# Flamingo block on Trainium2: the last key rows of a head group packed two heads to a score bank, the one left-over key apart, and x loaded turned

## The reference

```python
# x (8, 512, 256), ctx (8, 1601, 256), 16 heads of 16 channels
q, k, v = heads(layernorm(x) @ Wq.T), heads(ctx @ Wk.T), heads(ctx @ Wv.T)
attn = einsum('bhnc,bhlc->bhnl', q / 16, k)        # 512 queries x 1601 keys
attn = softmax(attn, axis=2)                       # over the QUERIES n, not the keys
attn = attn / attn.sum(axis=-1, keepdims=True)     # then over the keys
x = x + tanh(g_xattn) * (einsum('bhnl,bhlc->bhnc', attn, v) @ Wo.T)
# feed-forward: 8 experts, the best two of each token, hidden 1024, exact gelu
x = x + tanh(g_ffn) * moe(layernorm(x), router_w, w1, w2)
```

## Time and profile before

| | before |
|---|---|
| median of 3 runs | 1796.7 us (1795.38 to 1799.1) |
| the profiled execution, its own time | 1794.36 us |
| its span in the trace | 1792.6 us |
| busy PE, DVE, ACT, POOL over the span | 95%, 79%, 72%, 30% |
| attention, first exp to last exp | about 31 to 1230 us |
| one batch (2nd to 7th) | 151.3 us |
| granted TensorE clock | 0.996 |

### The profile page before, as it was taken

How to read it: one execution, slowest core, us unless ns; L and a number is a source line. 1 busy time by engine, 2 the same in 40 slices (tenths; PEclk the granted TensorE clock), 3 DMA queues, 4 the chain that set the end, 5 groups by cost and what they waited for, 6 DMA issues and landing times.

```text
span 1792.6 us, 31795 instructions
## 1 busy us (share of the span) xinstructions
PE 1703.8 (95%) x10074; PEld 918.3 (51%) x10074; DVE 1417.2 (79%) x2293; ACT 1283.0 (72%) x3653; POOL 538.2 (30%) x821
## 2 busy tenths in 40 slices
PE   8999999999999999999999999889999999999997
PEld 5233334333333433333333342225899999999997
DVE  7998999999999999999999999997344444444442
ACT  5999999999999999999999999996111111111111
POOL 3331252352343225235223422213122222222222
PEclk9999999999999999999999999999999999999999
DMA  8546226414712721551371163419222222222221
GB/s 231 139 121 183 66 70 158 129 40 123 187 47 62 198 72 52 158 154 40 102 187 51 51 172 75 154 52 326 67 37 35 36 37 35 38 35 35 36 37 27
DMA packets 128247, 172.90 MB, mean 96 GB/s; under 512 B 14496, under 2 KB 105760, under 8 KB 128128
## 3 DMA queue, kind: packets, MB, share of 16 engines
q1 hardware_dynamic: 113152, 150.51, 30.8%
q0 software_dynamic: 14144, 20.44, 6.6%
q10 hardware_dynamic: 832, 0.53, 0.1%
HBM read 117.96 MB, written 53.47 MB: 96 GB/s over the span
## 4 chain that ended last, share of the span: by engine, by line
ACT 40%; PE 30%; DVE 20%; issue 7%; DMA 2%; POOL 1%; SPq 0%; POOLq 0%; DVEq 0%; ACTq 0%
ACT w_all L934 37%; DVE negmax L1114 14%; PE scores L1507 14%; PE scores L1520 13%; ACT w_all L879 1%; ACT parts L870 1%; DVE resid L1009 1%; DMA out<-row_t,gate_token 1%; PE spare L1497 1%; DVE rz L1100 1%; PE scores L732 1%; PE spare L593 1%; DVE x L1025 1%; DVE stats L1133 1%; DVE stats L1143 0%
## 5 line engine op out<-in xcount | busy, mean ns | idle before, releaser
L934 ACT ACTIVATE w_all<-scores,negmax 128x512 f32<-128x512 f32 (+1 forms) x1664 | 1128.9, 778 | 19.9 <-DVE negmax L1114 15.4
L1114 DVE TENSOR_REDUCE negmax<-scores 128x2 f32<-128x1024 f32 (+1 forms) x832 | 1001.9, 1215 | 53.8 <-PE scores L732 47.4
L732 PE MATMUL scores<-q_stack,w_all 128*128 128x512 bf16 (+1 forms) x1664 | 532.9, 385 | 42.1 <-ACT w_all L934 34.3
L934 ACT ACTIVATION_READ_ACCUMULATOR w_all<-scores,negmax 128x1 f32 (+1 forms) x1664 | 495.2, 298 | 0.0
L745 PE MATMUL acc<-w_all,vz 128*32 128x512 f32 (+1 forms) x3328 | 443.7, 605 | 0.0
L732 PEld LDWEIGHTS scores<-q_stack,w_all 128*128 128x128 bf16 (+1 forms) x1664 | 136.8, 99 | 575.2 <-ACT w_all L934 514.6
L1553 ACT ACTIVATE projections<-scores 128x512 f32<-128x512 f32 x142 | 84.8, 597 | 445.8 <-PE scores L1507 440.2
L1337 POOL TENSOR_TENSOR vz<-w_all,rz 128x68 f32<-128x68 f32 (+1 forms) x416 | 124.5, 299 | 776.3 <-DVE rz L1100 751.0
L1507 PEld LDWEIGHTS scores<-row_t,q_stack 128*128 128x128 f32 x2272 | 264.4, 192 | 7.0 <-issue 2.0
L1507 PE MATMUL scores<-row_t,q_stack 128*128 128x128 f32 x2272 | 265.6, 275 | 1.9 <-DVE row_t L1580 1.9
L1520 PE MATMUL scores<-room,projections 128*128 128x256 f32 x1136 | 256.8, 379 | 0.0
(11 more groups left out here) (215 smaller groups left out, 1048.9 us busy)
## 6 DMA issues: line engine op xcount, KB each, us to landing
w_all<-k_parts SPq DMA_DIRECT2D x248, 200.1 KB, 3.5
w_all<-in_w SPq DMA_DIRECT2D x16, 1024.0 KB, 10.0
q_stack<-q_parts SPq DMA_DIRECT2D x248, 64.0 KB, 3.3
k_parts<-parts SPq DMA_DIRECT2D x42, 300.0 KB, 2.9
w_all<-in_ctx_t SPq DMA_DIRECT2D x7, 1601.0 KB, 7.1
parts<-routed SPq DMA_DIRECT2D x71, 129.0 KB
q_parts<-parts SPq DMA_DIRECT2D x14, 384.0 KB, 3.9
routed<-pad_row SPq DMA_DIRECT2D x8, 645.0 KB
```

The source lines that it names most:

```text
L732: mm = pe.matmul(scores[0:r, 2 * (u % SLOTS) + j % 2, :], k_stacks[g][:, j, lt * P:lt * P + r], q_stack[:, g, j, :], start=True, stop=True)
L934: act.activation(probs[0:r, s % RING, j, :], scores[0:r, 2 * (u % SLOTS) + j % 2, :], ACT.Exp, bias=negmax[0:r, u % 4, j % 2:j % 2 + 1], a ...
L1114: dve.tensor_reduce(negmax[0:r, u % 4, :], scores[0:r, 2 * (u % SLOTS):2 * (u % SLOTS) + 2, :], AX.X, ALU.max, negate=True).then_inc(negma ...
```

## The change

It does four things.

1. **Packing.** The last tile now holds 64 rows. A group's 13th step is one unit: the four heads' scores are made by four matmuls with 64 columns, heads 0 and 1 (2 and 3) one above the other in one bank. Key 1600, left over, is put apart for all 16 heads at once: one more unit of one bank (the *lone* unit), in which row 32j + g is head j of group g, made by 16 matmuls with 32 columns. Batch 0 makes it in two parts, at steps 12 and 38, the others in one, at step 12. `weigh` of each 13th step has four more matmuls for it. The numbering of slots runs on over the batches.
2. **Values.** The last v piece (tiles 12 and 13) is made with the new shapes, and DVE takes it with a multiplication by a 0/1 mask (`own_rows`), where ACT copied it. It is now at step 24.
3. **x.** x is given turned as well and loaded so (`x_t`). SP writes means and deviations to DRAM, loads them back on all partitions, and POOL centres and scales `x_t` at steps 24 to 27. The two x_turn pieces are gone.
4. **The table.** Steps 12, 25, 38 and 51 carry no side work. v 0 to 5 stand at 36, 41, 43, 45, 47 and 49. `load_ctx` waits for v 5 (step 49) and no longer for v 6 (step 47).

```diff
-LT = (L + P - 1) // P
+LT = L // P
+LAST_TILE = LT * P
+REST = L - 1 - LAST_TILE
+TAIL_ROWS = 32
+LONE = LAST_TILE + REST
+LONE_AT = LONE + H // 4 - 1
+LK = LONE_AT + TAIL_ROWS
+VT = LT + 2
+GROUP_STEPS = LT + 1
...
 FILL_AT = {
     1: ("next", "k", 0), 3: ("next", "k", 1), 4: ("tail", "o_turn", 3), 5: ("tail", "attn_turn", 1),
...
+    7: ("tail", "out_proj", 0), 9: ("tail", "out_proj", 1), 11: ("next", "k", 2),
+    14: ("next", "k", 3), 16: ("next", "k", 4), 17: ("cur", "o_turn", 0), 18: ("tail", "row_turn", 0),
+    19: ("tail", "row_turn", 1), 21: ("tail", "logits", 0), 23: ("next", "k", 5), 24: ("next", "v", 6),
+    27: ("next", "k", 6), 29: ("next", "k", 7), 30: ("cur", "o_turn", 1), 32: ("next", "q", 0), 34: ("next", "q", 1),
+    36: ("next", "v", 0), 37: ("cur", "attn_turn", 0),
+    39: ("tail", "prefix", 0), 41: ("next", "v", 1), 43: ("next", "v", 2), 45: ("next", "v", 3), 47: ("next", "v", 4),
+    49: ("next", "v", 5), 50: ("cur", "o_turn", 2),
 }
...
+def lone_groups(b, g):
+    if b == 0:
+        return range(g, g + 2) if g % 2 == 0 else range(0)
+    return range(G) if g == 0 else range(0)
+
+def units_of(b, s):
+    g, lt = s // GROUP_STEPS, s % GROUP_STEPS
+    return 2 if lt < LT or len(lone_groups(b, g)) else 1
...
+        def spread_x_stats(it):
+            b = it.b
+            sp.wait_ge(rstd_step, 2 * (b + 2))
+            for s, stat in ((0, mv1[:, :, 0]), (1, rstd1[:, 1, :])):
+                sp.dma_start(x_stats_dram[s].rearrange("(t p) -> p t", p=P), stat, allow_slow_non_contiguous=True).then_inc(x_stats_stored, 16)
+
+        def gather_x_stats(it):
+            b = it.b
+            wait_apart(sp, x_stats_stored, 32 * (b + 1), passed_sp)
+            sp.dma_start(x_stats[:, :, :], x_stats_dram.partition_broadcast(P)).then_inc(x_stats_in, 16)
...
         def load_ctx(it):
 
-            sp.wait_ge(fill_taken, it.made("v", VF - 1))
+            sp.wait_ge(fill_taken, it.made("v", VF - 2))
             sp.dma_start(ctx_sb[:, :, :], ctx_rows[it.b + 2]).then_inc(ctx_loaded, 16)
...
+            elif p == 0:
+                for j in range(GH):
+
+                    wait(pe, exp_done, 2 * (u - SLOTS) + j // 2 + 1)
+                    mm = pe.matmul(scores[REST * (j % 2):REST * (j % 2 + 1), bank + j // 2, :],
+                                   k_stacks[g][:, j, LAST_TILE:LAST_TILE + REST], q_stack[:, g, j, :], start=True, stop=True)
+            else:
+                groups = lone_groups(b, g)
+
+                wait(pe, exp_done, 2 * (u - SLOTS) + 1)
+                for of in groups:
+                    for j in range(GH):
+                        mm = pe.matmul(scores[32 * j:32 * j + TAIL_ROWS, bank, :],
+                                       k_stacks[of][:, j, LONE_AT - of:LONE_AT - of + TAIL_ROWS], q_stack[:, of, j, :],
+                                       start=(of == groups[0]), stop=(of == groups[-1]))
...
+            if lt == LT:
+                pe.wait_ge(lone_vz_ready, lone_units(b, g))
+                for j in range(GH):
+                    mm = pe.matmul(acc[32 * j:32 * j + DH + 1, :], lone_vz[:, g * GH + j, :], lone_probs[:, :],
+                                   start=False, stop=True)
...
+            elif name in ("v", "own_v"):
+                dve.tensor_tensor(v_ones[(b + 1 if name == "v" else b) % 2][:, LT:VT, :, 0:DH],
+                                  spare[:, :].rearrange("p (t h c) -> p t h c", t=2, h=H),
+                                  own_rows[:, :, :].unsqueeze(3).to_broadcast([P, 2, H, DH]), ALU.mult).then_inc(fill_taken, 1)
...
+                if it.next and s in (SHIFT_X, SHIFT_X + 1):
+                    k = s - SHIFT_X
+                    if k == 0:
+                        wait_apart(pool, x_t_loaded, (b + 1) * 16, passed_pool)
+                        pool.wait_ge(x_stats_in, (b + 1) * 16)
+                    pool.tensor_tensor(x_t[:, k, :], x_t[:, k, :], x_stats[:, 0, :], ALU.subtract).then_inc(centred1, 1)
```

More of the change, by code:

```diff
@@ L54 @@
 KCHUNK = 4
-KCOLS = [(L * i) // KCHUNK for i in range(KCHUNK + 1)]
+KCOLS = [(LK * i) // KCHUNK for i in range(KCHUNK + 1)]
 KCMAX = max(KCOLS[i + 1] - KCOLS[i] for i in range(KCHUNK))
 CHUNKS = KC + KC * KCHUNK
-VF = (LT + 1) // 2
+VF = VT // 2
 TOKENS = B * N
@@ L111 @@
 CENTRE_X = 17
+SHIFT_X = 24
 class Iteration:
@@ L649, in fill @@
                 wait(pe, fill_taken, it.made(name, i) - 1)
-            if name == "x_turn":
-                pe.wait_ge(xn_ready, 2 * (b + 2))
-                mm = turn_x(spare, i)
-            elif name == "q":
+            if name == "q":
+                if i == 0 and 0 in halves:
+                    pe.wait_ge(xn_ready, 2 * (b + 2))
                 mm = project_q(spare, i, halves)
@@ L952, in _ @@
         dve.wait_ge(dve_setup, DVE_SETUP)
+        own = Chain(dve, own_rows_step, 0)
+        own(dve.memset(own_rows[:, :, :], 0.0))
+        own.settle()
+        own(dve.memset(own_rows[0:REST, 0, 0::2], 1.0))
+        own(dve.memset(own_rows[REST:P, 0, 1::2], 1.0))
+        for g in reversed(range(G)):
+            for j in range(GH):
+                own(dve.memset(own_rows[32 * j:32 * j + g + 1, 1, g * GH + j:g * GH + j + 1], 1.0))
+            own.settle()
+            if g:
+                for j in range(GH):
+                    own(dve.memset(own_rows[32 * j:32 * j + g, 1, g * GH + j:g * GH + j + 1], 0.0))
+        own.settle()
+        for tiles in v_ones:
+            own(dve.tensor_copy(tiles[:, LT:VT, :, DH], own_rows[:, :, :]))
+        own.settle()
         def bc(ap):
@@ L1125, in run @@
                     f = it.fill(s)
-                    if f and f[0] not in ("v", "own_v", "x_turn") and p == (f[0] in ("q", "k")):
+                    if f and (f[0] not in ("v", "own_v") or f in LAST_V) and p == (f[0] in ("q", "k")):
                         take(it, *f)
```

248 lines of the change are left out of this document (143 added, 105 removed).

## The result

The changed kernel takes 1834.1 us (median of four executions, 1831.8 to 1838.3) where the kernel before took 1796.1 in the same job: a ratio of 1.0208, with a 95% interval of 1.0195 to 1.022. It is 38 us slower. 1783.7 was forecast, with a range of 1766 to 1803, so both the sign and the range were missed. The profiled execution took 1838.29 by its own time, 4.2 above the median, for a span of 1836.6. Against the 1794.4 of before it is 43.9 us longer, and that is the sum to be explained here.

What follows compares the result with a forecast made beforehand. ACT was taken as the bound, with little room behind it. Middle batches -8, first -1.9, last -4.4 and ends +1.2 made -13: 1794.4 to 1781.4, plus 2.3 for the median, 1783.7 us; range 1766 to 1803.

Steps and rivals of the forecast that it cites:

- So 2.0 us of waiting, in each change of batch: Change of batch: context lands at 7.8 us, PE stands from 4.4, ACT waits 2.0 us, at six changes.
- 5 if in 10: Upper end of ACT's wait per change of batch: 5 us if the context load takes 10 us to land.
- the same sign comes if the context takes 10 us to land: Rival at the change of batch: a context landing in 10 us also makes the kernel slower; within slower's 0.19.
- slower: Case that the changed kernel takes longer than before: chance 0.19, of which the lone matmuls 0.10.
- I cost it nothing: Turned x: statistics stored and reloaded through DRAM, bounded by 14 us where POOL has 18, priced at no time.
- 0.35 (0 to 1.1 ...): Step 24: DVE's masked copy of v 6 waits for PE and precedes its second reduce, 0.35 us per batch.
- DVE's sum (0.7): Steps 25 to 30: DVE has some 16.3 us against ACT's 15.3; 0.7 us per batch, between 0 and 1.3.
- the lone key at 28 (0.6): Step 28: the longer `weigh` delays the second unit's scores by a little more than 0.5 us.
- the price of the lone key in `weigh`: Four more matmuls at steps 15, 28, 41 and 2: 1.7 us per middle batch, 0.4 to 4.
- the rival that had them in turn: Step 12: the 16 lone matmuls run one after another, 3.5 us on PE, total 1803; chance 0.10.
- The running slots: Change of batch: slots that run on remove a 0.7 us wait, seven restarts, 4.9 us in all.
- The rival that all waits stay covered (-50): Whole kernel: ACT's saved work and the slot restarts count in full, -50, 1747 us; waits covered had chance 0.21.

Runs made afterwards that it cites:

- a2: Changed kernel with the context loaded in two halves, the first after v 3 and the rest after v 5: 1806.32 us, ratio 1.0051 to the kernel before.
- b1: Kernel before with the turned x alone, without packing or running slots: 1798.99 us against 1795.68, ratio 1.0017.
- b4: Kernel before with v 6 moved from step 47 to 49, so that its context load is issued two steps later: 1805.89 us, ratio 1.0059.
- c1: b2 with the first half of the context issued ahead of the last stack loads in the first batch: 1785.53 us against 1794.62, ratio 0.9952.
- a1: Changed kernel with the fourth group's stack loads waiting until the context has landed: 1826.47 us, ratio 1.0169 to the kernel before.
- a3: Changed kernel with POOL's four operations on the turned x cut from 512 to 8 columns, all waits kept: 1826.42 us, ratio 1.0167 to the kernel before.
- b2: a2 with x by rows and turned by PE as before, and v 6 at step 38 behind its second unit: 1795.49 us, ratio 1.0.
- b3: a2 without the four matmuls that add the lone key in each 13th step's `weigh`: 1793.23 us, ratio 0.9989 to the kernel before.
- c3: Kernel before with only the slots' numbering running on over the batches: 1784.45 us, ratio 0.9946.

## Why the prediction failed

In the profiled execution the sum is off by 57 us (-13 forecast, +43.9 measured). By terms:

| term | forecast | measured | off by |
|---|---|---|---|
| step 0 of the six changes of batch | +12 | +33.7 | 21.7 |
| steps behind them (1 to 3) and single late steps | 0 | +5 | 5 |
| the six batches without both, against 151.3 each | -20 (148.0 each) | -2 (151.0 each, by a2) | 18 |
| first batch | -1.9 | +6.7 | 8.6 |
| last batch | -4.4 | -3.1 | 1.3 |
| ends | +1.2 | +3.4 | 2.2 |

The terms are read from one execution of each kernel. In that of the kernel before, the clock is at half for 3.4 us at the start of the last batch, and its step 0 takes 4.01 where b1 and b4 show 2.87; without this the last batch's gain would be about 2 and not 3.1. Of the ends no run shows the cause: c1, with the same packing, has only 0.2 more than before behind the last exp.

**The context, the largest error.** The mechanism was named and priced ("So 2.0 us of waiting, in each change of batch"), and the size was wrong: 5.6. Three things were missing. The 7.1 us of the earlier trace rows were measured where no other transfers were on the way; the moved load has the fourth group's 16 stack transfers issued 3.4 us behind it and lands in 7.5 to 11.1 (a1: 7.2 without them). The clock after the wait was left out. Where it is at half, it doubles the time of k 0 and what follows (b4: 1.67 for 0.83), and by the estimate above it is the largest part, 10 of the 21.7. And the first batch was taken like the others, where SP comes to the load late (c1: 5.2 us there alone). The end of the price's range, "5 if in 10", was passed by the mean, though five of the six loads landed in under 10 (median 8.3): by the prediction's own sum 8.3 would make 3.2. The rival "the same sign comes if the context takes 10 us to land" named the right term, though the sign came with less. It had the 0.09 that slower held beside the lone matmuls, and should have had most of the chances.

**The turned x, costed at nothing.** "I cost it nothing" failed twice. In the middle batches POOL's four operations hold up DVE's small ones with two operands (1316 ns against 181), 1.65 us per batch by a3. POOL's own take 1.27 with or without them. The Trainium skill ("SBUF — State Buffer", Who interferes with whom) says that a DVE instruction with two inputs in SBUF contends with a GpSimd one that reads SBUF, over a pair of ports that the two engines share under an exclusive lock; the traces agree, as the DVE instruction of 0.18 us ended with POOL's of 1.27. In the first batch, which b2 makes 8.3 us shorter than a2, the stores stand ahead of k's. The prediction cites the Trainium skill ("DMA: Bandwidth & Descriptors", Rules for kernel authors) for a strided last dimension that becomes one descriptor per element. The trace agrees, with 1088 packets under 512 bytes between 88 and 101 us, where the two stores have 1024 elements. The time is 11.9 us for both stores in the first batch, 12.4 in the fifth (726.34 to 738.70), 9.7 to 13.2 over the seven. The chain of stores and load was bounded by 14 ("far larger") and judged harmless, since POOL had 18. It took 16.9 us in the first batch and 16.1 in the fifth, so the bound was wrong; POOL indeed did not wait. What was not asked is who is queued with it: the store of a k piece, whose buffer ACT needs. Alone on the kernel before, the turned x costs 3.3 us (b1).

**The middle batches.** By the steps' lengths, less 0.661 for each exp and ACT's copies, ACT waits 5.6 us in a batch before and 11.1 in a2. Where the difference lies, and what the terms of the forecast put there:

| steps | forecast | measured |
|---|---|---|
| 0 to 10 | +0.3 | +0.25 |
| 11 to 13 | 0 | +0.2 |
| 14 to 23 | +0.5 | +0.5 |
| 24 (v 6) | +0.35 | +1.07 |
| 25 to 30 | +1.45 | +3.6 |
| 31 to 50 | +0.45 | +0.2 |
| 51 | -0.55 | -0.3 |
| sum | +2.5 | +5.5 |

Two rows hold the error. "0.35 (0 to 1.1 ...)" for v 6 came out at its upper bound, for a reason that wasn't weighed: PE may start the piece only when DVE has taken k 5's rest, and needs 2 us for it. In steps 25 to 30 the forecast is DVE's sum (0.7), the lone key at 28 (0.6) and a one-unit step (0.15). POOL's part, 1.65 by a3, was missing, and the sum itself was 0.5 too small.

**What was right.** 1609 exps; the price of the lone key in `weigh` (1.7 per batch by b3, in sum though not step by step); no wait of POOL for the statistics; and the 16 lone matmuls, which lie side by side. The groups of the whole run with the lone unit's matmuls (32 columns) and the packed scores (64):

```profile
L821 PE MATMUL scores<-q_stack,w_all 128*32 128x512 bf16 x128 | 8.6, 381 | 3.1 <-ACT w_all L1022 3.1
...
L813 PE MATMUL scores<-q_stack,w_all 128*64 128x512 bf16 x128 | 19.9, 391 | 0.0
```

The 128 lone matmuls of all batches took 8.6 us, 1.1 for 16; the rival that had them in turn is out. The running slots were under-sized: 4.9 forecast, 10.2 by c3, of which 7.9 lies in the batches. The 0.7 of the last step came as said (3.38 to 2.65); missing were 0.44 in steps 2 and 3 of each middle batch, and 1.0 in the last batch is the half clock of the kernel before and not the slots' (b1 and b4, whose slots restart, have the shorter last batch too).

**Where the gain of the packing went.** ACT's 5.8 us per batch were counted as time, with single waits set against them. c1 and c3 bear on this: both have the running slots, x as before and no wait for a context, and differ in the packing and in where the context's load and v 6 stand. They are 1.1 us apart (1785.5 and 1784.5), less than can be told. The 4.9 us of work that ACT is spared per batch come back as 5.1 of waiting for DVE and PE. By the steps' lengths these lie in steps 0 to 10 (0.7, the lone key), 11 to 23 (0.6), 25 to 30 (1.4), 31 to 50 (1.9) and 51 (0.4). Of the 1.9 nearly all is v 6 in the one-unit step 38 and what follows at 41: 1.8 more there than in a2, which has v 6 at 24, where it costs 1.07. So part of what the packing loses is a matter of the table; a better place for v 6 with x by rows was not tried, and these runs don't show that the packing could never gain. The rival that all waits stay covered (-50) was as wrong as the forecast.

What stays open: what the packing gives with v 6 in another place; where 1.4 of c3's gain outside the batches comes from; and why the store of k behind the statistics lands in 8.5 us in one run and 10.4 in another.

## What to carry to other kernels

When three engines are each within 5% of the period, work taken from one may come back as its waiting, as 4.9 us per batch did here: price a saving by an experiment that only removes it, and look first at waits that belong to no engine's work, such as a slot numbering that begins anew, which gave 10 us here for an edit of a few lines. A load that is moved is priced with the transfers that share its time, the place in its issuer's queue in the irregular first round, and the lower clock that PE may have after a wait: it came at five of six changes, and where it came, a wait of 2.80 cost 4.8 us. A transfer is not free because its reader has time: ask what is stored behind it and whose buffer that holds.

## What the hardware showed unasked

- A DVE multiplication of 128x32 with two operands in SBUF took 1316 ns beside POOL's 128x512 operation with two full operands, 181 without; 503 where the two overlapped in part (b1). POOL's operation takes 1.27 us (1.267 to 1.283 over 28 of them), beside DVE's or not; one that centres by rows took 1.04.
- At five of the six changes of batch PE's granted clock was 0.50, for 3.4 to 10.2 us, behind waits of 2.80 to 9.26; behind one of 3.08 it stayed at 1.00. In b4 it was at half behind waits of 1.03 and 1.42 and full behind 0.61, 0.73 and 0.82; behind the wait of 1.42 the next matmuls took 1.67 for 0.83.
- Two stores of 2 KB each in elements of 4 bytes took 9.7 to 13.2 us until both had landed, over seven batches; a store of k issued behind them in the first batch landed in 8.5 to 10.4 us, in 3.5 where they were absent (b2).
- bf16 matmuls of 32 or 64 columns that lie side by side overlap as the f32 ones of the earlier trace rows do.
